# A fused attention and int8-fake-quant FFN layer: up-projection matmuls moved into the FFN-1 loop, quantization chunks shifted from phase 4 to phase 3

## What is computed

```python
def fake_quant_weight(w, bits=8):
    qmax = 2.0 ** (bits - 1) - 1
    scale = jnp.max(jnp.abs(w)) / qmax
    wq = jnp.clip(jnp.round(w / scale), -qmax - 1, qmax) * scale
    return w + jax.lax.stop_gradient(wq - w)

def qat_lora_linear(x, W, b, A, B):      # W: (o, i), A: (16, i), B: (o, 16)
    base = einsum('bsi,oi->bso', x, fake_quant_weight(W)) + b
    lora = einsum('bsr,or->bso', einsum('bsi,ri->bsr', x, A), B)
    return base + 2.0 * lora

h = qat_lora_linear(x, W_fc, ...)        # 1024 -> 4096
h = gelu(h)
h = qat_lora_linear(h, W_proj, ...)      # 4096 -> 1024
```

## Time and profile before

| | us |
|---|---|
| median of 2 runs | 2213.93 (2180.01 and 2247.85) |
| the profiled execution | 2178.26 |
| its span on the slowest core, first to last instruction | 2176.7 |
| spans of the other cores | 2164.2 to 2175.8 |

### The profile page before, as it was taken

One profiled execution on the slowest core, in us unless ns is written; L12 is line 12 of the kernel. 1 busy time (PEld: TensorE's weight loads), 2 busy tenths in 40 slices (PEclk: granted clock), 3 DMA queues, 4 the chain that ended last, 5 costly groups with the idle time before them and its releaser, 6 DMA issues.

```text
span 2176.7 us, 28282 instructions; the slowest of 8 cores (2164.2 to 2176.7 us)
## 1 busy us (share of the span) xinstructions
PE 1346.7 (62%) x7038; PEld 681.7 (31%) x7038; DVE 1019.1 (47%) x1325; ACT 881.8 (41%) x1229; POOL 74.9 (3%) x119
## 2 busy tenths in 40 slices
PE   0073676776767767467222204358989889898795
PEld 0020122222222222123000102125756556574563
DVE  2247677777777777754557555542020111201112
ACT  0000266666666666323560056652332423324231
POOL 0000000000000001000000000000000000000000
PEclk9575788788886887679555655558989889898897
DMA  6410011212112214212220033320000000000000
GB/s 183 135 42 0 8 60 51 69 61 66 49 61 66 60 52 161 102 40 77 76 80 0 27 106 92 102 68 13 9 21 1 20 6 16 20 1 20 1 20 20
DMA packets 51901, 112.28 MB, mean 52 GB/s; under 512 B 12656, under 2 KB 23408, under 8 KB 50464
## 3 DMA queue, kind: packets, MB, share of 16 engines
q0 software_dynamic: 13552, 50.08, 7.1%
q1 hardware_dynamic: 28688, 37.06, 5.7%
q10 hardware_dynamic: 9504, 23.34, 3.7%
HBM read 97.47 MB, written 8.39 MB: 49 GB/s over the span
## 4 chain that ended last, share of the span: by engine, by line
PE 40%; DVE 23%; ACT 17%; DMA 11%; issue 8%; DVEq 1%; ACTq 1%; SPq 0%; POOLq 0%
PE PSD L313 33%; DVE CL L692 6%; ACT PT L699 5%; ACT QSG L802 4%; PE BIG L608 3%; DVE MXW L565 3%; PE PSD L676 3%; DMA QSG<-wPRr 3%; DMA QSG<-wFCr 3%; DVE CL L685 2%; ACT QTI L806 2%; DMA STG<-xT 1%; ACT TSQ L1186 1%; DVE XT L1051 1%; DVE XFM L1044 1%
## 5 line engine op out<-in xcount | busy, mean ns | idle before, releaser
L313 PE MATMUL PSD<-XT,RTF 128*128 128x256 bf16 x2048 | 310.0, 302 | 148.7 <-ACT HH L1134 146.4
L699 ACT ACTIVATE PT<-CL 128x1024 bf16<-128x1024 f16 (+1 forms) x320 | 310.8, 971 | 184.2 <-DVE CL L685 89.8
L692 DVE TENSOR_SCALAR CL<-PSD 128x1024 f16<-128x1024 f32 x192 | 235.1, 1225 | 74.5 <-PE BIG L608 32.7
L676 PE MATMUL PSD<-QH,KH 96*128 96x512 bf16 (+3 forms) x640 | 202.3, 409 | 108.0 <-DVE CL L685 49.2
L313 PEld LDWEIGHTS PSD<-XT,RTF 128*128 128x128 bf16 x2048 | 196.2, 106 | 223.8 <-issue 166.1
L608 PE MATMUL BIG<-PT,VP 128*65 128x512 bf16 (+3 forms) x640 | 201.0, 402 | 66.1 <-ACT PT L699 53.7
L313 PE MATMUL PSD<-HH,RTP 128*128 128x256 bf16 x2048 | 234.6, 273 | 6.4 <-DVE UPt L1151 6.4
L313 PEld LDWEIGHTS PSD<-HH,RTP 128*128 128x128 bf16 x2048 | 195.2, 98 | 37.0 <-issue 8.4
L802 ACT ACTIVATE QSG<-QSG,SML 128x512 f32<-128x512 f32 x128 | 104.1, 813 | 251.3 <-DMA QSG<-wFCr 144.8
L1134 ACT ACTIVATE HH<-PSD,BFCS,SML 128x256 bf16<-128x256 f32 x256 | 144.3, 564 | 147.9 <-PE PSD L313 133.8
L685 DVE SCALAR_TENSOR_TENSOR CL<-PSD,TRI 128x896 f16<-128x896 f32 (+1 forms) x128 | 122.7, 958 | 44.0 <-PE BIG L608 22.5
(11 more groups left out here) (148 smaller groups left out, 1331.2 us busy)
## 6 DMA issues: line engine op xcount, KB each, us to landing
STG<-wFCr POOLq DMA_DIRECT2D x32, 512.0 KB, 4.3
STG<-wPRr POOLq DMA_DIRECT2D x32, 512.0 KB, 4.4
out<-OST SPq DMA_DIRECT2D x64, 128.0 KB, 1.8
QSG<-wFCr ACTq DMA_DIRECT2D x27, 256.0 KB, 2.7
QSG<-wFCr POOLq DMA_DIRECT2D x26, 256.0 KB, 3.0
QSG<-wPRr SPq DMA_DIRECT2D x22, 256.0 KB, 3.0
QSG<-wPRr POOLq DMA_DIRECT2D x21, 256.0 KB, 2.9
QSG<-wPRr ACTq DMA_DIRECT2D x21, 256.0 KB, 2.7
```

The costliest lines, as they stand in the source:

```text
L313: e.matmul(outap, la, ra, start=st, stop=sp),
L676: e.matmul(self.PSD[pslot][:, 512 * half: 512 * half + qext], self.KHB[b][0:96, 128 * kt:128 * kt + 128], self.QHB[b][0:96, qlo:qlo + qext ...
L692: e.tensor_scalar(self.CLB[cs][:, 0:qw], self.PSD[pslot][:, 0:qw], 80.0, -80.0, ALU.min, ALU.max),
L699: etok = P.s(lambda e, cs=cs, qw=qw: e.activation(self.PTB[cs][:, 0:qw], self.CLB[cs][:, 0:qw], AF.Exp, scale=ISQ), waits=[ctok, self.pv_t ...
```

## The change

Three places are edited.

1. In phase 3 a chunk is emitted after each of the four groups of a slice, in place of the first two: 32 chunks in the phase in place of 16.
2. In phase 4 two chunks are emitted in a slice in place of four: 16 in the phase in place of 32. The total before phase 5 is 48 as before.
3. In FFN-1 each of the 32 up-projection matmuls is emitted directly behind the GELU of its block (in TensorE's list: behind the block), and waits for that GELU. The accumulation into `PSB[2]` stays open over the 32 blocks. The call in front of FFN-2 goes, and the scaling into UPt waits for the last of the 32.

```diff
@@ phase3
                 self.ps_free[sl] = ytok
                 self.y_tok[(dslice, nb)] = ytok
-                if nb < 2:
-                    self.emit_quant_chunk()
+                self.emit_quant_chunk()
@@ phase4
-            for _ in range(4):
-                self.emit_quant_chunk(allow_pr=False)
+            self.emit_quant_chunk(allow_pr=False)
+            self.emit_quant_chunk(allow_pr=False)
@@ phase5
                 self.ps_free[sl] = hh_tok[oc]
+                upw = [hh_tok[oc], self.apt_r]
+                if oc == 0:
+                    upw.append(self.ps_free[2])
+                upmm = P.t(lambda e, oc=oc, t=t: e.matmul(
+                    self.PSB[2][0:16, 0:TC],
+                    self.APT[:, 16 * oc:16 * oc + 16],
+                    self.HH[:, TC * oc:TC * oc + TC],
+                    start=(oc == 0), stop=(oc == 31)),
+                    waits=upw, inc=(oc == 31))
                 if self.quant_sched or self.q_inflight:
                     self.emit_quant_chunk()
                     self.emit_quant_chunk()
             while self.quant_sched or self.q_inflight:
                 self.emit_quant_chunk()
-            sl = 2
-            mmtok = self.mmg(
-                self.PSB[sl][0:16, 0:TC],
-                [(self.APT[:, 16 * f:16 * f + 16], self.HH[:, TC * f:TC * f + TC])
-                 for f in range(32)],
-                [self.apt_r, self.ps_free[sl]] + [hh_tok[oc] for oc in range(32)])
-            up_tok = P.v(lambda e, sl=sl: e.tensor_scalar(
-                self.UPt[0:16, 0:TC], self.PSB[sl][0:16, 0:TC],
-                self.SML[0:16, 4:5], None, ALU.mult), waits=[mmtok])
-            self.ps_free[sl] = up_tok
+            up_tok = P.v(lambda e: e.tensor_scalar(
+                self.UPt[0:16, 0:TC], self.PSB[2][0:16, 0:TC],
+                self.SML[0:16, 4:5], None, ALU.mult), waits=[upmm])
+            self.ps_free[2] = up_tok
```

## The result

| | us |
|---|---|
| changed kernel, median of 11 runs | 2715.29 (2712.87 to 2733.37) |
| before, median of 10 runs beside them | 2198.26 (2178.24 to 2247.85) |
| ratio of the undisturbed runs | 1.243, 95% interval 1.2386 to 1.2474 |
| profiled execution after (before: 2178.26) | 2713.58 |
| its span on the slowest core | 2712.0 |

In some executions, those of the kernel before above all, the cores of one die run at a lower clock and the time is longer; the ratio is taken from the others. The change makes the kernel 24% slower. Forecast were 2668 us, in a range of 2540 to 2750.

What follows compares the result with a forecast made beforehand. TensorE alone was taken to bound FFN tiles 1 to 7. From the profiled 2178.3 us, 450 (FFN-1) + 0 (tile 0) + 18 (FFN-2) + 56 (phase 3) - 34 (phase 4) = +490 gave 2668 us, stated range 2540 to 2750.

Steps and rivals of the forecast that it cites:

- The wait puts the next block behind the GELU: FFN-1: in-order TensorE holds the next block behind the up-projection matmul waiting for the GELU, 32 times a tile.
- FFN-1 runs at 1.2 GHz throughout: FFN-1, tiles 1 to 7: the lower clock level holds for all of it; chance 0.77.
- the rival at 2.4 GHz: FFN-1 at the high clock throughout: pitch 2.34 us, seven tiles +222 us, total 2422 us; chance 0.07.
- Pitch 3.39 us: FFN-1: time from block to block at 1.2 GHz, 3.18 us of chain plus 0.21 for the up-projection matmul.
- The term of the sum that was put at 450: FFN-1 of tiles 1 to 7: 64.3 us longer a tile, 450 us for seven, bounds 430 to 485.
- FFN-2 starts low, 2.3 us a tile: Start of FFN-2: it begins at 1.2 GHz and loses 2.3 us; 18 us over eight tiles (0 to 30).
- Tile 0 costs nothing: FFN-1 of tile 0: added matmuls hidden behind late ScalarE; +3.9 and -5.0 us at the end, together about 0.
- Phase 3 +56 us: Phase 3: a second pair of chunks in the slice's circle costs 8 x 7.0 us, +56 (44 to 74).
- Phase 4 -34: Phase 4: with fewer chunks the YC1 circle sets 8.2 us a slice, -34 us (-22 to -38).
- signs named: Signs of being right, among them: FFN-1 105 to 115 us, WOBs casts 17 to 19 us apart, YC1 casts 8 to 9.
- the swinging clock: FFN-1: the clock goes up and down, pitch 2.87 us, seven tiles +337 us, total 2549 us; chance 0.12.
- The case in which the wait costs nothing: FFN-1: TensorE starts the next block while the up-projection matmul waits, overlap stays, total 2200 us; chance 0.03.

Runs made afterwards that it cites:

- up_lag2: Changed kernel with each up-projection matmul emitted two blocks later, reading a GELU two blocks old: 2213.29 us, ratio 1.0156 to before.
- up_fill10: Changed kernel plus ten unread filler matmuls between each block and its up-projection matmul in tiles 1 to 7: 2481.72 us (one run).
- quant_only: Kernel before with only the quantization chunks moved (phase 3: four a slice, phase 4: two), up-projection unchanged: 2193.67 us, ratio 1.0079.
- up_only: Kernel before with only the up-projection matmuls moved behind their blocks, chunks unchanged: 2695.32 us, ratio 1.2373.

## Why the prediction was right

- *The wait puts the next block behind the GELU:* right, as line 1142's 240 waits show, and shown to be the cause by up_lag2.
- *FFN-1 runs at 1.2 GHz throughout:* right, 0.50 in the stretch. It was the largest choice, worth 228 us between the cases of 2.34 and 3.39 us a block, and had been made by likeness to tile 0, whose gaps were longer (4.16 us); no row of before could decide it, so this part of the hit rests on a guess with a reason. up_fill10 shows the other side at 2482 us, 60 above the 2422 of the rival at 2.4 GHz; its pitch of 2.59 in place of 2.34 is 31 x 7 x 0.25 = 54 us of these.
- *Pitch 3.39 us:* low; it is 3.60, outside the bounds of 3.3 to 3.55 that I gave. 0.10 is the order of the waits, 0.09 the matmul's neighbours. FFN-1 is 117.7 us in place of 110.7; 7 x 7.0 = 49 us. The term of the sum that was put at 450, with bounds of 430 to 485, measured 7 x 71.2 = 498. That is about the miss of the whole (2714 in the profiled execution against 2668), since the misses of the other terms nearly cancel. I had called the row's 0.15 the price of a hand-over, without looking at how many waits the receiving instruction had, and in which order.
- *FFN-2 starts low, 2.3 us a tile:* 2.1 measured, 17 us in place of 18.
- *Tile 0 costs nothing:* right within 1 us.
- *Phase 3 +56 us:* +58.7. *Phase 4 -34:* -39.5, outside the bounds of -22 to -38; the circle of YC1 closes in 7.5 us, quicker than the 8.2 put together from rows. The two misses, 2.7 and 5.5 us, go opposite ways, so that the sum, +19 against +22, looks better than its terms; quant_only's +17 confirms it.
- *Range:* 2715 lies inside the 2615 to 2745 added up from the bounds, but two of the terms lie outside their own. Room that the other terms did not need held the total, which is luck. Of the signs named, the length of FFN-1 (117.7 against 105 to 115), the casts of WOBs (19.4 apart against 17 to 19) and those of YC1 (7.5 against 8 to 9) each came just outside.
- *The rivals:* the swinging clock did not come (0.50 without a rise in 116 us). The Trainium skill's rule on it, in "TensorE: Matmul & The Clock Gate", section "A second HAM failure mode: psum-queue depth-cycling" (short idles between groups make the gate swing), is not what this pattern does: with TensorE idle for 1.1 us behind every block it stayed at the lower level. The case in which the wait costs nothing fell with the first trace. The Trainium skill's finding in "TensorE: Matmul & The Clock Gate", section "HAM oscillation — how this bites in real kernels", that double buffering in PSUM gave no further gain, doesn't carry over: here the same two halves were kept, the overlap was lost, and the kernel was 24% slower for it (up_only, 1.2373).

## What to carry to other kernels

On an engine that works its list in order, a matmul that reads the newest result of another engine takes away the overlap that the buffers gave; ask for the result two steps later and the overlap is back (here 94% of the excess). Where such a wait comes behind every block, look at the granted clock as well: here it stayed at 0.50, which added 1.01 us a block to the 1.40 us of the wait itself. Write the wait that is met last as the last one, keep small matmuls of another tile shape together, and when work is moved beside a loop, look for the circle in which it will stand and not for the idle time of its engine.

## What the runs showed of the hardware that was not expected

- A wait long met, placed behind the one that is late, costs 0.10 us each time (0.25 against 0.15 us from the GELU's end to TensorE's start).
- A 128x16 matmul between ones of other shapes takes 0.21 us at full clock, and 0.11 in a run of its kind. The surplus goes with the change of shape, not with a wait, the open accumulation or the PSUM part written.
- FFN-1 begins at the lower clock level, and with TensorE idle for 1.1 us behind every block the granted clock stayed at 0.50 through its 117.7 us, in all the tiles 1 to 7.
- Adding 2240 matmuls to the changed kernel made it 232 us faster (one run), by way of the granted clock (0.50 to 0.98 in the stretch).
